# A graph network layer: the edge sums of the next group in two parts, one between the halves of layer one

## What is computed

```
msg = relu(x[src] + edge_attr)                      # one row per edge
h   = x + segment_sum(msg, dst)                     # one row per node
h   = relu(relu(h @ W1 + b1) @ W2 + b2)             # 128 -> 256 -> 128
out = layernorm(x + h)                              # no scale, no shift, eps 1e-5
```

## Time and profile before

| | |
|---|---|
| median of 3 runs | 460.35 us (459.53 to 460.59) |
| the profiled execution | 459.55 us |
| its span, first to last instruction | 457.9 us |
| mean granted TensorE clock | 0.999 |
| busy: TensorE matmuls, weight loads | 98%, 83% |
| busy: VectorE, ScalarE, GpSimd | 95%, 86%, 80% |

### The profile page before, as it was taken

The page is one execution under the profiler, slowest core; times in us unless marked ns, Lnnn a source line. Parts: engine busy times, 40 slices in busy tenths (PEclk is TensorE's granted clock), DMA queues, the critical chain, the costliest instruction groups (busy, mean ns, idle before and its releaser), DMA issues.

```text
span 457.9 us, 10648 instructions
## 1 busy us (share of the span) xinstructions
PE 449.9 (98%) x3033; PEld 378.0 (83%) x3033; DVE 433.3 (95%) x1759; ACT 394.2 (86%) x929; POOL 368.4 (80%) x403
## 2 busy tenths in 40 slices
PE   7999999999999999999999999999999999999995
PEld 5888888888888888888888888888888888888884
DVE  6799999999999999999999999999999999999996
ACT  4599888898888889988888888888888888888886
POOL 7777888888888888768888888888888888888842
PEclk9999999999999999999999999999999999999999
DMA  5586666666666666666666666666666666666632
GB/s 137 160 236 198 198 185 200 199 194 199 187 198 203 178 199 203 182 198 197 197 202 188 201 194 196 185 200 201 197 194 196 192 197 205 187 198 194 197 126 89
DMA packets 83871, 86.82 MB, mean 190 GB/s; under 512 B 12024, under 2 KB 79509, under 8 KB 83813
## 3 DMA queue, kind: packets, MB, share of 16 engines
q1 hardware_dynamic: 75044, 68.77, 48.5%
q0 software_dynamic: 8496, 17.38, 14.1%
q10 hardware_dynamic: 272, 0.00, 0.0%
HBM read 60.51 MB, written 25.60 MB: 188 GB/s over the span
## 4 chain that ended last, share of the span: by engine, by line
PE 97%; DVE 1%; DMA 1%; ACT 1%; issue 0%; SPq 0%; DVEq 0%
PE h_ps L1007 38%; PE h1T_ps L999 37%; PE hT_ps L950 11%; PE hT_ps L945 9%; DMA dst_rows<-in_dst_dram 1%; PE prep_ps L450 0%; PE hT_ps L921 0%; DVE stats L692 0%; PE hT_ps L938 0%; PE hT_ps L971 0%; PE hT_ps L976 0%; DVE z L685 0%; ACT std L837 0%; ACT hT L826 0%; ACT h1T L832 0%
## 5 line engine op out<-in xcount | busy, mean ns | idle before, releaser
L134 POOL DMA_INDIRECT x_src<-in_x_dram,src_of x254 | 269.1, 1059 | 67.5 <-issue 59.4
L1007 PE MATMUL h_ps<-w_sb,h1T 128*128 128x128 f32 x1564 | 197.5, 276 | 0.0
L999 PE MATMUL h1T_ps<-hT,w_sb 128*128 128x384 f32 (+1 forms) x524 | 190.0, 485 | 0.3 <-ACT hT L826 0.3
L1007 PEld LDWEIGHTS h_ps<-w_sb,h1T 128*128 128x128 f32 x1564 | 185.2, 192 | 0.0
L832 ACT ACTIVATE h1T<-h1T_ps,b_sb 128x384 f32<-128x384 f32 (+1 forms) x262 | 151.0, 578 | 35.6 <-PE h1T_ps L999 27.3
L999 PEld LDWEIGHTS h1T_ps<-hT,w_sb 128*128 128x128 f32 x524 | 89.4, 191 | 35.0 <-issue 0.6
L851 ACT ACTIVATE y<-z,shift,rstd 128x128 f32<-128x128 f32 x263 | 114.6, 483 | 1.2 <-DVE shift L712 0.4
L592 POOL TENSOR_SCALAR y<-z,rstd,shift 128x128 f32<-128x128 f32 x123 | 87.3, 710 | 13.5 <-DVE shift L712 9.0
L950 PE MATMUL hT_ps<-sel,msg_hi 128*128 128x216 f32 x250 | 94.6, 446 | 0.0
L692 DVE BATCH_NORM_STATS2 stats<-z 128x6 f32<-128x128 f32 x391 | 88.6, 282 | 0.1
L945 PE MATMUL hT_ps<-ident,x_sb 128*128 128x128 f32 x375 | 87.5, 272 | 0.0
(11 more groups left out here) (123 smaller groups left out, 180.5 us busy)
## 6 DMA issues: line engine op xcount, KB each, us to landing
x_sb<-in_x_dram SPq DMA_DIRECT2D x130, 192.0 KB, 2.5
out_dram<-y SPq DMA_DIRECT2D x130, 192.0 KB, 2.5
pre_msg<-in_edge_attr_dram SPq DMA_DIRECT2D x130, 128.0 KB, 2.8
x_src<-in_x_dram,src_of POOLq DMA_INDIRECT x254, 3.0
w_sb<-in_w_dram SPq DMA_DIRECT2D x2, 128.0 KB, 2.6
dst_rows<-in_dst_dram SPq DMA_DIRECT2D x1, 97.7 KB
x_src<-in_x_dram,first_pairs POOLq DMA_INDIRECT x6, 2.8
b_sb<-in_b_dram SPq DMA_DIRECT2D x1, 64.0 KB, 3.2
```

What stands on the lines that cost most here:

```text
L134: nc.gpsimd.indirect_dma_start(out=c["x_src"][:, g % EB, k, :], out_offset=None, in_=x, in_offset=bass.IndirectOffsetOnAxis(ap=index, axis ...
L999: nc.tensor.matmul(h1T_ps[h][:, 0:n, 0:p], w1_sb[:, h * 128:(h + 1) * 128], hT[:, 0:n, 0:p], start=True, stop=True).then_inc(h1_summed, 1)
L1007: last = nc.tensor.matmul(h2_ps[g % 2][0:p, t, :], h1T[:, h, t, 0:p], w2_sb[:, h, :], start=(h == 0 and t == 0 and not biased(g, c)), stop ...
```

## The change

`sum_turned` is cut in two: `sum_high` (the waits for `sel`, `msg_hi` and `x`, then high, tile 0, high, tile 1) and `sum_low` (the wait for `msg_lo`, then low, tile 2, low, and the signal). `hidden_sum` takes the halves to do. For the groups g = 3 to 127 the order on TensorE is now: half 0 of layer one of g, the high half of the sums of g+1, half 1 of layer one of g, the low half of the sums of g+1, the output layer of g. The instructions and their number are the same. No other engine's list is touched.

```diff
-        def sum_turned(g):
...
+        def sum_high(g):
 
             pe.wait_ge(sel_ready, g - FIRST_GROUPS + 1)
             pe.wait_ge(msg_hi_ready, parts_to(g, c) + 1)
-            add(0, msg_hi, start=True)
+            add_chunk(g, 0, msg_hi, start=True)
             pe.wait_ge(x_loaded[g % XB], (g // XB + 1) * 16)
-            turn(0)
-            add(1, msg_hi)
-            turn(1)
+            turn_tile(g, 0)
+            add_chunk(g, 1, msg_hi)
+            turn_tile(g, 1)
+
+        def sum_low(g):
+
             pe.wait_ge(msg_lo_ready, parts_to(g, c) + 1)
-            add(0, msg_lo)
-            turn(2)
-            add(1, msg_lo, stop=True).then_inc(hT_summed, 1)
+            add_chunk(g, 0, msg_lo)
+            turn_tile(g, 2)
+            add_chunk(g, 1, msg_lo, stop=True).then_inc(hT_summed, 1)
...
-        def hidden_sum(g):
+        def hidden_sum(g, halves=range(HC)):
             p, n = partitions(g, c), tiles(g, c)
-            pe.wait_ge(hT_copied, g + 1)
-            for h in range(HC):
+            if 0 in halves:
+                pe.wait_ge(hT_copied, g + 1)
+            for h in halves:
...
         for g in range(3, GROUPS):
-            hidden_sum(g)
             if g + 1 < END:
-                sum_turned(g + 1)
-            elif inside(g + 1):
+                hidden_sum(g, (0,))
+                sum_high(g + 1)
+                hidden_sum(g, (1,))
+                sum_low(g + 1)
+            else:
+                hidden_sum(g)
+            if END <= g + 1 <= LAST:
                 turn_x(g + 1)
                 sum_messages(g + 1)
```

More of the change, by code:

```diff
@@ L940, in sum_messages, with turn_tile, add_chunk @@
             last.then_inc(hT_summed, 1)
-        def sum_turned(g):
[L944 to L951, removed]
+        def turn_tile(g, t):
+            nc.tensor.matmul(hT_ps[:, t, :], x_sb[:, g % XB, t, :], ident[:, :], is_transpose=True,
+                             start=False, stop=False, skip_group_check=True)
+        def add_chunk(g, k, part, start=False, stop=False):
+            cols = sel[:, g % EB, k, :].rearrange("p (t q) -> p t q", t=T)
+            return nc.tensor.matmul(hT_ps[:, 0:T, LO[k]:LO[k] + WP], part[:, g % EB, k, :], cols,
+                                    start=start, stop=stop, skip_group_check=True)
+        def sum_high(g):
             pe.wait_ge(sel_ready, g - FIRST_GROUPS + 1)
             pe.wait_ge(msg_hi_ready, parts_to(g, c) + 1)
-            add(0, msg_hi, start=True)
+            add_chunk(g, 0, msg_hi, start=True)
             pe.wait_ge(x_loaded[g % XB], (g // XB + 1) * 16)
-            turn(0)
-            add(1, msg_hi)
-            turn(1)
+            turn_tile(g, 0)
+            add_chunk(g, 1, msg_hi)
+            turn_tile(g, 1)
+        def sum_low(g):
             pe.wait_ge(msg_lo_ready, parts_to(g, c) + 1)
-            add(0, msg_lo)
-            turn(2)
-            add(1, msg_lo, stop=True).then_inc(hT_summed, 1)
+            add_chunk(g, 0, msg_lo)
+            turn_tile(g, 2)
+            add_chunk(g, 1, msg_lo, stop=True).then_inc(hT_summed, 1)
         def sum_first(i, final=False):
```

## The result

The changed kernel takes 500.56 us at the median of 6 runs (500.01 to 501.48), against 460.34 us of the kernel before (6 runs): a ratio of 1.088, 95% interval 1.087 to 1.089. Slower, as forecast; the forecast was 508 us in a range of 498 to 519.

A forecast was written before the change was run, and what follows sets the result against it. TensorE's passes bound the kernel at 3.38 us a group; a one-group loop through ScalarE's list would make it 3.76. 459.55 + 0.65 + 124 x 0.38 (47.1) = 507.3, or 508 us at the median, range 498 to 519.

The forecast's parts named there:

- The high half is late from the start: TensorE, first high sum: moved 0.65 us ahead, it wants `msg_hi` at 205.20, but `msg_hi` ends at 205.41.
- The loop's terms: Steps from relu of half 1 through ScalarE's list and TensorE to the next such relu: 3.76 us, chance 0.80.
- restart: TensorE, from the end of `msg_hi` to the first column streamed of the high half: 0.22 us, lower bound 0.16.
- The choice of 0.20 against 0.26: ScalarE, deviation to copy of hT: 0.20 us once sums are long done; the bare row's 0.26 kept as upper bound.
- The total: Whole kernel: 459.55 + 0.65 + 47.1 (124 periods x 0.38) = 507.3 us profiled, 508 against the median.
- the 0.65: First group (group 4): half 1 of layer one now stands behind the wait for `msg_hi`, costing 0.65 us once.
- TensorE's own work unchanged: TensorE: the same 23 passes, none added; seven sum passes still take 0.74 us.
- The gain of up to 1.3 us: TensorE: one more sum pass directly behind a long pass, 0.10 instead of 0.11; at most 1.3 us, counted as 0.
- Cover of the copy of hT and of `msg_lo`: Next layer one and low half: both operands ready in time, copy with 0.30 us of room; cost 0 to 0.05.
- The rival over VectorE: Two-group circle through output layer, bias, VectorE's edge sum and `msg_hi` sets the period: 3.61 us, about 489 us; chance 0.06.
- The weight load ahead of the wait: Rival on TensorE: the restart's load is hidden, 0.11 us; period 3.65, 495 us; chance 0.05.
- A falling clock: Part of the further-wait rival: granted clock falls in new gaps of about 0.4 us; over 519 us; chance 0.05, shared.

The follow-up runs named there:

- the run in which both lists are shortened: Changed kernel with ScalarE's `msg_hi` ahead of the second tile of y and VectorE's edge sum of g+3 ahead of selection and aggregates: 460.26 us, ratio 1.0008.

## Why the prediction was right, and where it was off

The direction, the place and the mechanism were as forecast, and the time was within the range but near its lower end, 7.4 us under the forecast. Step by step:

- *The high half is late from the start.* Right: every steady group takes 3.70 us or more, and the wait in it is 0.33 us long.
- *The loop's terms.* Relu to deviation 0.48 (forecast 0.48); deviation to copy 0.19 at the median of all groups (0.20); copy to first tile 0.37 (0.39); between tiles 0.39 (0.39); second tile to `msg_hi` 0.38 (0.38); `msg_hi` 0.41 (0.42); restart: `msg_hi` ends at 201.15, the turned tile behind the first high pass starts at 201.48, less 0.10: 0.23 (0.22); high half 201.38 to 201.80, 0.42 (0.43); half 1 to its relu 201.80 to 202.65, 0.85 (0.85). The sum is 3.72, the measured period 3.707, the forecast 3.76.
- *What was mis-sized* is thus the sum, by 0.053 us against the measured period, in small parts: 0.02 in the step from the copy, 0.01 each in the deviation, in `msg_hi` and in the high half, 0.01 the other way in the restart, and the rest in rounding. The copy of hT takes 0.48 instead of the 0.49 of the earlier trace rows when it isn't released by TensorE at that moment. Over 124 periods 0.053 us is 6.6 of the 7.4 us. A loop multiplies each rounding by the number of its turns.
- *The choice of 0.20 against 0.26* for the deviation step was right. The copy's start in the earlier trace rows was held by TensorE's sums; with the sums long done it follows after 0.19. Back-to-back instructions of ScalarE overlapped by 0.10 here (0.29 less 0.19), by about 0.093 in the Trainium skill ("ScalarE: Activation LUTs", "What ACT_TABLE_LOAD costs").
- *The total.* Between the groups 4 and 128 the mean period is 3.384 before and 3.707 after, and 459.55 + 0.65 + 124 x (3.707 - 3.384) = 500.25, against 500.48 of the profiled execution. The count of 124 periods holds. The first group cost 0.93 and not 0.65: in the chains layer one of group 4 starts at 25.37 before and at 26.30 after. Of that, 0.30 is that `msg_hi` ended at 23.19 and not at 22.89, as edge features landed later in this execution; the rest, 0.63, fits the 0.65.
- *TensorE's own work unchanged:* right, by the run in which both lists are shortened. The gain of up to 1.3 us didn't show.
- *Cover of the copy of hT and of `msg_lo`:* held. Layer one's loads have 1.5 us of idle time ahead of them in all, over 524 loads, by the page.
- *The rival over VectorE* was right as a circle, which the two runs with `msg_hi` moved show, and wrong in its price: 3.61 us forecast, 3.40 to 3.43 found, since its 3.53 from bias to edge sum was read at a place where VectorE was slower than in most groups (3.24 at the median of the kernel before). Its 489 us would have been 464.
- *The weight load ahead of the wait:* it didn't happen. The load starts 0.11 after the end of `msg_hi`, at 201.26, and by the same 0.11 in every group.
- *A falling clock:* it didn't fall, with 0.33 us of gap in every 3.71.

## What to carry to other kernels

Before an instruction with a fresh operand is moved ahead of one whose result the operand's engine waits for, follow the circle: sum start-to-start steps through every engine's written order back to the same instruction of the next turn. If the circle closes within one turn and is longer than the period, its excess is paid every time, even by an engine that is 74% busy; then shorten that list, or leave the order. Take each step from a place where it doesn't itself wait, compare it with the same step in other groups, and keep the third digit, for the loop multiplies it.

## What the runs showed of the hardware

In this kernel unlike passes in turn were cheaper than like passes in a row. An edge sum (216 columns) and a turned tile (128 columns) take 0.214 us as a pair; in blocks a turned tile takes 0.109 (0.33 for three) and an edge sum 0.11 (0.43 to 0.44 for four). That is 0.025 us a group and 2.8 to 2.9 us in all, with the split and without it. What makes the difference wasn't tried.

A wait of TensorE can hide in two views: in the chain it appeared as a first pass of 0.35 us, and in the list of waits as "issue" ahead of the load. The load's start next to ScalarE's records named it. Idle time ahead of a load is no proof of a wait of the matmul: 0.67 us of it stood ahead of the load with the wait, 0.29 without.
